# Perceiver layer on one core: the finish of the heads in three f16 passes, with Wv and Wo split on chip during the steps

## The reference

```
x = x + cross_attention(norm(x), ctx, Wq, Wk, Wv, Wo)   # 16 heads of 128
x = x + linear_attention(norm(x), ...)                  # 16 heads of 32, decay
x = x + ffn(norm(x), w1, b1, ln_g, ln_b, w2, b2)        # ternary weights, 8 bit rows
```

## Time and profile before

| | |
|---|---|
| median of 3 runs | 1971.22 us (1969.66 to 1971.35) |
| the profiled execution's own time | 1971.78 us |
| its span (what the profile covers) | 1970.0 us |
| TensorE busy | 1931.6 us (98%) |
| VectorE busy | 1594.3 us (81%) |
| ScalarE busy | 1139.9 us (58%) |
| mean granted clock of TensorE | 0.996 of full speed |

### The profile page before, as it was taken

One profiled execution on the slowest core, in us unless ns is written; L12 is line 12 of the kernel. 1 busy time (PEld: TensorE's weight loads), 2 busy tenths in 40 slices (PEclk: granted clock), 3 DMA queues, 4 the chain that ended last, 5 costly groups with the idle time before them and its releaser, 6 DMA issues.

```text
span 1970.0 us, 46349 instructions
## 1 busy us (share of the span) xinstructions
PE 1931.6 (98%) x17373; PEld 1582.4 (80%) x17373; DVE 1594.3 (81%) x3423; ACT 1139.9 (58%) x2517; POOL 268.7 (14%) x459
## 2 busy tenths in 40 slices
PE   7999999999999999999999999999999999999896
PEld 7877987977978987977978978977978978977762
DVE  7878878878888888888888888888888888787746
ACT  5766666656656565555656555565555655555423
POOL 1011111111111111111111111111111111100000
PEclk9999999999999999999999999999999999999998
DMA  7768878788877879887788878877787777876590
GB/s 216 151 137 163 163 160 174 147 166 159 162 146 144 142 142 175 152 158 153 148 156 158 154 147 162 162 156 152 149 164 153 146 140 138 151 134 131 128 337 6
DMA packets 966944, 304.44 MB, mean 155 GB/s; under 512 B 893984, under 2 KB 952864, under 8 KB 965824
## 3 DMA queue, kind: packets, MB, share of 16 engines
q1 hardware_dynamic: 966720, 301.47, 77.0%
HBM read 72.16 MB, written 4.46 MB: 39 GB/s over the span
## 4 chain that ended last, share of the span: by engine, by line
PE 92%; DVE 4%; ACT 1%; DMA 1%; issue 1%; SPq 0%; POOL 0%; ACTq 0%; DVEq 0%; POOLq 0%
PE ps_v L1367 25%; PE ps_s L1352 25%; PE ps_w L1367 19%; PE ps_t L1352 19%; DVE pp L1015 1%; PE ps_v L1339 1%; DMA bulk<-in_vo 1%; PE ps_w L1326 1%; PE ps_v L1466 0%; PE ps_t L1459 0%; PE ps_s L1502 0%; DVE prob L1010 0%; DMA pt<-pp 0%; PE ps_s L1299 0%; DVE acc L1023 0%
## 5 line engine op out<-in xcount | busy, mean ns | idle before, releaser
L1367 PE MATMUL ps_v<-nring,pt 128*128 128x256 f16 x4704 | 580.9, 273 | 1.0 <-ACT acc L649 0.4
L1352 PE MATMUL ps_s<-bulk 128*128 128x128 f16 (+2 forms) x4752 | 581.3, 271 | 0.1
L1367 PEld LDWEIGHTS ps_v<-nring,pt 128*128 128x128 f16 x4704 | 458.3, 98 | 61.7 <-ACT acc L649 1.3
L1352 PEld LDWEIGHTS ps_s<-bulk 128*128 128x128 f16 x4752 | 402.6, 98 | 111.6 <-DVE bulk L945 0.3
L1352 PE MATMUL ps_t<-bulk 128*128 128x384 f16 (+2 forms) x3564 | 452.4, 272 | 7.4 <-DVE mx L976 3.8
L1367 PE MATMUL ps_w<-nring,pt 128*128 128x256 f16 x3528 | 451.8, 273 | 3.3 <-ACT ps_w L701 1.2
L1015 DVE SCALAR_TENSOR_TENSOR pp<-prob,pp 128x384 f16<-128x384 f32 (+4 forms) x680 | 423.7, 689 | 0.6 <-ACT pp L695 0.6
L1367 PEld LDWEIGHTS ps_w<-nring,pt 128*128 128x128 f16 x3528 | 340.2, 98 | 51.7 <-ACT part_v L710 3.1
L1352 PEld LDWEIGHTS ps_t<-bulk 128*128 128x128 f16 x3564 | 300.4, 98 | 100.4 <-DVE mx L976 7.0
L695 ACT ACTIVATE pp<-prob 128x384 f16<-128x384 f32 (+4 forms) x680 | 371.1, 624 | 11.8 <-DVE prob L1010 6.3
L684 ACT ACTIVATE prob<-ps_s,nmax 128x768 f32<-128x768 f32 (+2 forms) x136 | 119.1, 875 | 429.1 <-DVE nmax L992 420.9
(11 more groups left out here) (212 smaller groups left out, 1386.8 us busy)
## 6 DMA issues: line engine op xcount, KB each, us to landing
stage<-in_ctx SPq DMA_DIRECT2D x196, 128.0 KB, 2.9
wst<-in_w SPq DMA_DIRECT2D x64, 256.0 KB, 3.2
bulk<-in_vo SPq DMA_DIRECT2D x16, 512.0 KB, 5.5
pt<-pp SPq DMA_TRANSPOSE x272, 5.7
tern_d<-wter SPq DMA_DIRECT2D x32, 128.0 KB, 3.0
bulk<-tern_d SPq DMA_DIRECT2D x2, 2048.0 KB, 20.7
acc<-in_qk SPq DMA_DIRECT2D x6, 512.0 KB, 5.5
nring<-in_aw SPq DMA_DIRECT2D x3, 1024.0 KB, 12.4
```

Of the source, the lines that this page charges most:

```text
L1352: ins = mm(out if n == 1 else out.rearrange("p (n m) -> p n m", m=P), q_part(e, qlo, a)[:, c * P:(c + 1) * P], t_moving(k, run, tlo, b, c) ...
L1367: ins = mm(dst, pt[:, tile:tile + P], n_part(c, clo, b), start=(first and n == 0 and plo == 0 and clo == 0), stop=(last and n == w - 1 and ...
```

## The change

1. Two weight sums run in a step instead of one, in steps 10 to 25.
2. In steps 28 to 59 (`VO_AT`) one half-head piece of Wv or Wo per step (128 x 512, f32) is loaded to `wst`, split by ScalarE into a high f16 half and by VectorE into a low one, both in the buffer `halves`, which is the memory of `wter`, and stored to `vo16_d` in DRAM.
3. Rounding of the ffn weights moves to steps 62 to 125.
4. In the finish, the normalized values are split before the turning (ScalarE the high half, VectorE the low one), the turning takes eight f16 blocks, the products with Wv and Wo take three f16 passes each, and the outputs are split by VectorE (`o_copy`, two operations). The reciprocals are taken for two heads at once (`norm_pair`). ScalarE normalizes heads 0 and 1 before its last step.

The diff, cut to its core:

```diff
-        ABS_AT, QUANT_AT = 10, 50
+        ABS_AT, VO_AT, QUANT_AT = 10, 28, 62
...
+            def load_halves(m):
+                if m >= 2:
+                    sp.wait_ge(vo_lo, m - 1)
+                else:
+                    sp.wait_ge(w_abs, 2 * WP - 1 + m)
+                sp.dma_start(wst[:, (m % 2) * D:(m % 2 + 1) * D],
+                             vo_d[Q_ORDER[m // 2]][:, (m % 2) * D:(m % 2 + 1) * D]).then_inc(in_w[m % 2], 16)
+            def store_halves(m):
+                sp.wait_ge(vo_lo, m + 1)
+                sp.dma_start(vo16_d[m], halves).then_inc(out_v, 16)
...
             for k in range(1, NS + 1):
                 turn_p(k - 1, 0)
                 turn_p(k - 1, 1)
                 for c in range(1, NCH):
                     if SPLIT_AT[c] == k - 2:
                         turn_n(c)
...
-                if 0 <= k - ABS_AT + 1 < 2 * WP:
-                    load_w(k - ABS_AT + 1)
+                if 0 <= k - ABS_AT + 1 < WP:
+                    load_w(2 * (k - ABS_AT + 1))
+                    load_w(2 * (k - ABS_AT + 1) + 1)
+                if 0 <= k - VO_AT - 1 < 2 * H:
+                    store_halves(k - VO_AT - 1)
+                if 0 <= k - VO_AT + 1 < 2 * H:
+                    load_halves(k - VO_AT + 1)
...
@@ ScalarE, step(k), behind the weight sums and ahead of exp_head(k, 0) @@
+                if 0 <= k - VO_AT < 2 * H:
+                    m = k - VO_AT
+                    act.wait_ge(in_w[m % 2], 16 * (WP + m // 2 + 1))
+                    if m:
+                        act.wait_ge(out_v, 16 * m)
+                    nc.scalar.activation(halves[:, 0:D], wst[:, (m % 2) * D:(m % 2 + 1) * D], ACT.Copy,
+                                         scale=W_SCALE).then_inc(vo_hi, 1)
...
-            for k in range(NS):
+            for k in range(NS - 1):
                 step(k)
+            def norm_hi(f):
+                act.wait_ge(rl_scaled, f // 2 + 1)
+                if f >= 2:
+                    act.wait_ge(ut_mm, f - 1)
+                else:
+                    act.wait_ge(lo_done, 5 * (NS - 1))
+                nc.scalar.activation(un_part(f, 0), acc_of(Q_ORDER[f]), ACT.Copy, scale=rl[:, f % 4:f % 4 + 1]).then_inc(un_hi, 1)
+            norm_hi(0)
+            norm_hi(1)
+            step(NS - 1)
...
@@ VectorE, step(k), behind the sums of probabilities @@
+            def halves_lo(k):
+                m = k - VO_AT
+                if not 0 <= m < 2 * H:
+                    return
+                v.wait_ge(vo_hi, m + 1)
+                nc.vector.scalar_tensor_tensor(halves[:, D:2 * D], wst[:, (m % 2) * D:(m % 2 + 1) * D], W_SCALE,
+                                               halves[:, 0:D], ALU.mult, ALU.subtract).then_inc(vo_lo, 1)
...
+            def norm_lo(f):
+                v.wait_ge(un_hi, f + 1)
+                nc.vector.scalar_tensor_tensor(un_part(f, 1), acc_of(Q_ORDER[f]), rl[:, f % 4:f % 4 + 1], un_part(f, 0),
+                                               ALU.mult, ALU.subtract).then_inc(un_lo, 1)
...
@@ TensorE, finish(f) and add_out(f) @@
-                    last = mm(ps_t[:, (f % 2) * D:(f % 2) * D + HD], w[:, half * HD:(half + 1) * HD],
-                              ut[:, (f % 2) * D + c * P:(f % 2) * D + (c + 1) * P], start=(c == 0), stop=(c == KC - 1))
+                    for wlo, ulo in ((0, 0), (0, 1), (1, 0)):
+                        last = mm(ps_t[:, (f % 2) * D:(f % 2) * D + HD], w[:, wlo * D + half * HD:wlo * D + (half + 1) * HD],
+                                  u[:, ulo * D + c * P:ulo * D + (c + 1) * P], start=(c == 0 and wlo == 0 and ulo == 0),
+                                  stop=(c == KC - 1 and wlo == 1))
...
+                for olo, wlo in ((0, 0), (0, 1), (1, 0)):
+                    last = mm(ps_u[:, :], ot_part(f, olo), w[:, (2 + wlo) * D:(3 + wlo) * D], start=(f == 0 and olo == 0 and wlo == 0),
+                              stop=(f == H - 1 and olo == 1), skip_group_check=True)
```

More of the change, by code:

```diff
@@ L33 @@
 P_SCALE = 2.0 ** 14
+U_SCALE = 16.0
+W_SCALE = 64.0
+O_SCALE = 64.0
 EXP_SCALE = float(HD) ** -0.5 / (CTX_SCALE * Q_SCALE)
@@ L145, in perceiver_layer @@
         SL = 2 * D
-        un, ut, ot = prob[:, 2 * D:4 * D], prob[:, 4 * D:6 * D], part_u[:, 0:3 * P]
+        un, ut, ot = (t.bitcast(F16) for t in (prob[:, 2 * D:4 * D], prob[:, 4 * D:6 * D], part_u[:, 0:3 * P]))
+        halves = wter[:, :].bitcast(F16)
         VO, NVO = TRW + 3 * QSW, 8
@@ L278, in vo_slot, with un_part, ot_part @@
         def vo_slot(f):
-            return ring_vo[:, (f % NVO) * SL:(f % NVO + 1) * SL]
+            return ring_vo[:, (f % NVO) * SL:(f % NVO + 1) * SL].bitcast(F16)
+        def un_part(f, lo, n=1):
+            at = (f % 2) * 2 * D + lo * D
+            return un[:, at:at + n * D]
+        def ot_part(f, lo):
+            at = (f % 3) * 2 * P + lo * P
+            return ot[:, at:at + P]
         def last_step(e):
@@ L295, in perceiver_layer @@
         out_w = [sem(f"out_w{k}") for k in range(2)]
+        vo_hi = sem("vo_hi")
+        vo_lo = sem("vo_lo")
+        out_v = sem("out_v")
         in_tern = sem("in_tern")
@@ L371, in perceiver_layer @@
         rl_done = sem("rl_done")
-        un_done = sem("un_done")
+        rl_scaled = sem("rl_scaled")
+        un_hi = sem("un_hi")
+        un_lo = sem("un_lo")
+        o_hi = sem("o_hi")
         ut_mm = sem("ut_mm")
@@ L761, in step @@
                     split_hi(k)
[L762 to L766, removed]
+                if 0 <= k - ABS_AT < WP:
+                    for n in (2 * (k - ABS_AT), 2 * (k - ABS_AT) + 1):
+                        piece = wst[:, (n % 2) * D:(n % 2 + 1) * D]
+                        act.wait_ge(in_w[n % 2], 16 * (n // 2 + 1))
+                        nc.scalar.activation(piece, piece, ACT.Abs, accum_out=wabs[:, n:n + 1]).then_inc(w_abs, 1)
+                if 0 <= k - VO_AT < 2 * H:
[5 more added lines that the diff above has]
+                                         scale=W_SCALE).then_inc(vo_hi, 1)
                 exp_head(k, 0)
@@ L823, in _ @@
                     value_e_u(NS - 4 + f)
+                if f + 2 < H:
+                    norm_hi(f + 2)
                 if f == 8:
@@ L1132, in _, with norm_pair @@
                 step(k)
-            def norm_head(f):
-                h = Q_ORDER[f]
+            def norm_pair(p):
+                h = Q_ORDER[2 * p]
                 final = last_step(h // 2)
+                factors = rl[:, 2 * (p % 2):2 * (p % 2) + 2]
                 v.wait_ge(l_done, 2 * alphas(final))
@@ L1163, in _ @@
                 if f + 2 < H:
-                    norm_head(f + 2)
+                    if f % 2 == 0:
+                        norm_pair(f // 2 + 1)
+                    norm_lo(f + 2)
                 o_copy(f)
@@ L1465, in add_out @@
                 pe.wait_ge(o_cp, f + 1)
-                mm(ps_u[:, :], ot[:, (f % 3) * P:(f % 3 + 1) * P], w[:, D:2 * D], start=(f == 0), stop=(f == H - 1),
-                   skip_group_check=True).then_inc(out_mm, 1)
+                for olo, wlo in ((0, 0), (0, 1), (1, 0)):
+                    last = mm(ps_u[:, :], ot_part(f, olo), w[:, (2 + wlo) * D:(3 + wlo) * D], start=(f == 0 and olo == 0 and wlo == 0),
+                              stop=(f == H - 1 and olo == 1), skip_group_check=True)
+                last.then_inc(out_mm, 1)
             turn(0)
```

65 lines of the change are left out of this document (41 added, 24 removed).

## The result

The changed kernel takes 2182.16 us (median of three runs, 2179.36 to 2188.36) against 1971.22 before: a ratio of 1.108 [1.1065, 1.1095]. The forecast was 2167 us. The profiled execution is the slowest of the three, 2188.36 us with a span of 2186.6.

The account below looks back on a forecast made before the run. TensorE, busy 98% of the span, was taken to bound the kernel. 1971.8 us plus 158 of stalls, 36 of clock and 2 of finish and last step gave 2167.8, by the median 2167 us; range 2115 to 2220.

Parts of the forecast that it names:

- The mechanism: Steps 28 to 59: ScalarE's copy waits for the previous store, making the exponential late and stalling TensorE in 31 steps; 0.93.
- Landing, 3.2 us: Splitting steps: time for the 256 KB store to land, taken from the load issued in the same place.
- the forecast's 158: Splitting steps: TensorE's stalls summed, 19 steps of 3.4 us plus 12 with a turning of context of 7.8 us.
- The plain stall: Splitting steps without a turning of context: TensorE stalls 3.4 us at the second value group, in 19 steps.
- Clock, 36 us: Behind the stalls: TensorE's clock falls, 1.7 us for each of 12 long stalls and half of 19 plain ones; bounds 0, 64.
- second clock rival: Splitting steps: the clock falls in every stalled step and returns late, 64 us in place of 36, 2195 us; chance 0.25.
- Last step, +2.3 us: Last step: score copy 3.5 us late behind ScalarE's normalizing, while VectorE's normalizations leave the path; about 2.3 us remain.
- Handoffs, 1.4 us: Finish: values pass ScalarE, then VectorE, before the turning; 1.4 us (0 to 3) where the last two steps' values are interleaved.
- Three passes, -1.8 us: Finish: f16 products save 0.45 us per head, but only 1.8 us is kept, behind the arrival of Wv and Wo.
- the place that the forecast named: Finish: TensorE's wait for the loads of Wv and Wo, at 1895.07 us before the change, expected to remain.
- Finish and last step: End of the kernel: 2.3 + 1.4 - 1.8 = +2 us, bounds -5 and +5.

Follow-up runs that it names:

- store_first: The changed kernel with the store of the halves issued ahead of the two turnings of the probabilities instead of behind them: 1975.1 us, 1.0029 of the kernel before.
- factors_once: store_first with the reciprocals of all heads taken in two goes instead of one go per pair in the loop of heads: 1971.43 us, 1.0007.
- decay_late: store_first plus two-go reciprocals, heads 0 and 1 normalized earlier, aw_q loaded earlier, and the decay exponential and mask products moved behind the heads: 1967.61 us, 0.9987.
- context_behind: The changed kernel with the store behind both turnings of the probabilities but ahead of the turning of context: 2120.59 us, 1.0756 of the kernel before.

## Why the prediction was right, and where its sizes were off

**The mechanism held, step by step.** The copy waits for its own store in 31 steps, the store stands behind the turnings, the second value group waits for ScalarE's copy, twelve steps pay for the turning of context too, and the stall repeats without wearing off. Steps before 28 and after 60 kept their pace: when step 28 begins the changed kernel is 0.9 us ahead of the one before, after the 31 steps it is 211.4 us behind, and so it stays up to the last step. store_first is the proof: the same work with the store ahead has none of it.

**Landing, 3.2 us.** It was 2.7 by the median and 2.84 by the mean. The mean counts for a sum over 31 steps: 31 x 0.36 = 11 us less, so the forecast's 158 becomes 147, and the trace has 144.2 us of waits. The plain stall also came out a little high in the forecast: by its own rows it is 473.28 - 470.06 = 3.2 us, and it was 3.1. I took the load issued in this place, 3.2; the load still takes 3.3. Here the rule of the Trainium skill cited in the forecast (its estimate 2.6) was nearer than the row chosen, though its figures are for DMAs issued from GpSimd. That stores land sooner than loads isn't shown: 128 KB stores from the same buffer take 3.0 us in this kernel, and the 256 KB ones take 2.0 to 4.1, with a median of 2.9, in store_first. What decides within that spread stays open.

**Clock, 36 us: the step that was mis-sized.** I let half of the plain stalls pay 1.7 us and the long ones 1.7 each. In the trace the slow products cost 62 us, 2.0 per step, and 67 with the ends of the rows in front of the stalls; holding the clock up was worth 44 to 51. In the step of 521.33, five groups of nine took 7.39 us, nearly three of them at half clock, where they take 4.92 at full clock: 2.5 us lost. The clock fell in 27 of the 31 steps, in all twelve long ones and in 15 of the 19 plain ones, and a fall cost 1.4 to 2.9 us: the forecast's second clock rival (64 us for this term, 2195 us with the landing it assumed) comes close to what happened. With waits and clock as measured the sum is 1971.8 + 144 + 67 + 5 = 2188, the profiled execution; it closes because the 67 is what the waits leave. Against the profiled execution the errors are -14, +31 and +3. The two large ones partly cancelled in the 2167: that it came within 15 us of the median is in part luck.

**Last step, +2.3 us.** +2.8 from the step's beginning to the first value product behind it (4.37 us before, 7.21 after), and the wait is the one named, for ScalarE's score copy: TensorE's longest wait grew from 1.46 to 3.61 us, 2.15 of the 2.8. The other 0.7 us is the half clock behind it, which the forecast had left out here.

**Handoffs, 1.4 us.** 3.6 up to the first addition of a head. About 2 of these are clock and not handoffs: the first six value products took 1.40 us where the same six take 0.65 at full clock, and the second head's turnings, its products and the values behind them took 3.5 where store_first takes 2.2. What is left, about 1.6, is near the count.

**Three passes, -1.8 us.** From the first addition on it is 1.2 us less (31.0 and 29.8), but not as argued. No wait for the loads was left, where one was expected: VectorE's reciprocals between the low halves kept the heads at 1.8 and 2.9 us in turn. Only when they were gone (factors_once) did the load bind, at the place that the forecast named. Finish and last step: +5.2 us against +2, at the bound of the range; without the clock it would be about +2.5.

## What to carry to other kernels

A store that frees a single buffer must go out ahead of the long instructions of its queue: here 32 stores of 0.57 us cost 10.5% behind transposes that hold the queue for 6.5 to 10.8 us, and nothing measurable ahead of them. When a side job is put into a gap, follow its buffer once round (store, landing, the copy that waits, and what is queued behind that copy), and add for each stall the time that TensorE's clock takes from the products behind it. Work saved in a stage that a load ends is kept only if the load comes earlier: each wait removed in the finish brought the next one up, and taking engine work away ahead of a late load (decay_late) gave nothing. A landing's median isn't enough where every step waits for it: sum it by the mean.

## What the runs showed of the hardware

Stalls of 2.2 to 4.1 us, once a step of 17 to 21 us, can bring TensorE from 2.4 to 1.2 GHz as well as the long ones: the granted clock fell behind 15 of 19 of them in the change and behind all twelve of 6.7 to 7.5 us, and I had expected half of the short ones to be spared. The length of the stall alone doesn't tell: four of 2.66 to 2.96 us were spared, and one of 2.17 wasn't. Over the loop's window the granted clock was 0.86, with longer and shorter stalls together, and 0.93 in context_behind, where all are short. Behind a stall of 6.76 us, five groups of nine products lost 2.5 us.

Unused products in the gap make the kernel 2% faster: 1.108 [1.1065, 1.1095] became 1.0856 [1.084, 1.0873] with 142 us of such products added.

A store of 256 KB from SBUF landed in 2.7 us (median; 2.3 to 4.4) where a load of the same size, issued a moment later, took 3.3, and one of 64 KB in 2.1 (2.0 to 4.1). With its place in the queue the same store's median changed to 2.9, from 2.0 to 4.1 us.

Two DMA transposes of 24 and 18 blocks of 128 x 128 held SP's queue for 6.5 us and one of 28 blocks for 4.3, and the store queued behind them went out less than 0.1 us after their end.
